# Attention: one unit in 15 of the 16 teams gets its exponentials on VectorE, in 20 steps spread over the team

## What is computed

```python
q = (x @ w_q.T).reshape(B, S, H, hd).transpose(0, 2, 1, 3)   # 16 heads of 16
...
scores = jnp.einsum('bhqd,bhkd->bhqk', q, k) / jnp.sqrt(jnp.float32(hd))
mask = prefix_lm_mask(NUM_PATCHES, S)                        # causal, first 196 keys open to the first 196 queries
scores = jnp.where(mask == 0, jnp.float32(-jnp.inf), scores)
attn = jax.nn.softmax(scores, axis=-1)
ctx = jnp.einsum('bhqk,bhkd->bhqd', attn, v)
```

## Time and profile before

| what | us |
|---|---|
| median of 3 runs (2373.08 to 2379.14) | 2374.06 |
| profiled execution, its own time | 2377.52 |
| its span | 2375.8 |
| start of the first and of the last exponential of attention | 217.1, 1252.8 |
| one team (start of the second to start of the third) | 64.7 |

### The profile page before, as it was taken

One profiled execution on the slowest core, in us unless ns is written; L12 is line 12 of the kernel. 1 busy time (PEld: TensorE's weight loads), 2 busy tenths in 40 slices (PEclk: granted clock), 3 DMA queues, 4 the chain that ended last, 5 costly groups with the idle time before them and its releaser, 6 DMA issues. The chain is left out here.

```text
span 2375.8 us, 37728 instructions
## 1 busy us (share of the span) xinstructions
PE 2127.9 (90%) x14197; PEld 1307.5 (55%) x14197; DVE 1303.1 (55%) x2070; ACT 1776.9 (75%) x2250; POOL 700.5 (29%) x700
## 2 busy tenths in 40 slices
PE   5995999999999999999995984999999999999920
PEld 4773333333333333333334873888888888888820
DVE  4663222222222222222224966988888888888848
ACT  4664999999999999999993762555566666666624
POOL 1111000000000000000001533887166666666631
PEclk9997999999999999999997976999999999999965
DMA  6886644555555544444503864888566767777558
GB/s 194 297 304 171 117 87 87 100 100 100 100 98 99 72 83 86 89 86 61 71 10 113 267 193 164 294 288 290 196 165 171 171 171 170 171 171 177 127 135 316
DMA packets 204264, 365.79 MB, mean 154 GB/s; under 512 B 18680, under 2 KB 141176, under 8 KB 195256
## 3 DMA queue, kind: packets, MB, share of 16 engines
q1 hardware_dynamic: 161084, 299.38, 46.9%
q0 software_dynamic: 34256, 55.20, 12.4%
q10 hardware_dynamic: 8748, 8.85, 1.2%
HBM read 219.81 MB, written 143.42 MB: 153 GB/s over the span
## 5 line engine op out<-in xcount | busy, mean ns | idle before, releaser
L959 ACT ACTIVATE att_prob<-att_scores 128x1024 f32<-128x1024 f32 (+2 forms) x1152 | 1022.6, 1047 | 38.2 <-PE att_scores L910 31.0
L929 PE MATMUL att_out<-att_prob,att_va 128*32 128x512 f32 (+3 forms) x5120 | 591.0, 543 | 14.7 <-DVE att_prob L991 14.7
L910 PEld LDWEIGHTS att_scores<-att_qs,att_ks 50*128 50x128 f32 x2560 | 213.1, 185 | 500.9 <-ACT att_prob L959 427.6
L910 PE MATMUL att_scores<-att_qs,att_ks 50*128 50x512 f32 (+3 forms) x2560 | 469.8, 433 | 18.3 <-DMA att_qs<-guard 17.0
L991 DVE SCALAR_TENSOR_TENSOR att_prob<-att_prob,att_tri 128x512 f32<-128x512 f32 x224 | 144.8, 688 | 613.4 <-ACT att_prob L959 613.4
L1485 POOL DMA_INDIRECT sums<-moe_y,moe_token x156 | 346.3, 2220 | 224.7 <-ACT moe_y L1641 189.1
L1548 PE MATMUL moe_ps<-moe_xt_hi,moe_w_hi 128*128 128x512 f32 x880 | 347.4, 395 | 0.0
L1548 PE MATMUL moe_ps<-moe_xt_hi,moe_w_lo 128*128 128x512 f32 x880 | 347.0, 394 | 0.0
L1548 PE MATMUL moe_ps<-moe_xt_lo,moe_w_hi 128*128 128x512 f32 x880 | 345.3, 392 | 0.0
L862 POOL DMA_DIRECT2D ctx_scr<-att_cout x64 | 48.3, 755 | 994.6 <-DVE att_cout L1009 954.1
L929 PEld LDWEIGHTS att_out<-att_prob,att_va 128*32 128x32 f32 x5120 | 111.3, 108 | 189.4 <-issue 96.3
(11 more groups left out here) (193 smaller groups left out, 3041.8 us busy)
## 6 DMA issues: line engine op xcount, KB each, us to landing
moe_wraw<-w_experts SPq DMA_DIRECT2D x55, 1412.0 KB, 6.6
qk_parts<-proj_qk SPq DMA_DIRECT2D x64, 512.0 KB, 4.2
att_qs<-qk_parts SPq DMA_DIRECT2D x180, 128.0 KB
att_ks<-qk_parts SPq DMA_DIRECT2D x180, 128.0 KB
rows_in<-att_zeros SPq DMA_DIRECT2D x13, 1548.0 KB, 21.0
moe_xin<-rows_in SPq DMA_DIRECT2D x39, 516.0 KB, 4.3
proj_xin<-x SPq DMA_DIRECT2D x16, 512.0 KB, 3.9
v_scr<-proj_va SPq DMA_DIRECT2D x16, 512.0 KB, 3.5
```

The lines of the kernel that those rows point to most:

```text
L910: last = nc.tensor.matmul(pss[e % SBUFS][:, h, at:at + CH - q0], ks[s][rows, half, kt * P:(kt + 1) * P], qs[s][rows, half, c * CH + q0:(c ...
L929: last = nc.tensor.matmul(pso[k % 2][strip, q0:], va[team % 2][:, kt, strip], prob[u % PBUFS][:, h, at:at + CH - q0], start=(kt == 0), sto ...
L959: nc.scalar.activation(prob[u % PBUFS][:, half * 2:half * 2 + 2, start:], pss[e % SBUFS][:, :, start:], ACT.Exp, scale=HD ** -0.5)\
```

## The change

`LATE` names unit 22, the second key tile of the last chunk, in teams 1 to 15. It leaves the ring of units. Its scores are computed behind those of unit 11, half a team earlier, in the same three score buffers and in turn with the others. Its two halves are not exponentiated on ScalarE: VectorE does it with 10 instructions for each half, 20 in all, as a power of two (scale and clamp out of PSUM, round, shift the integer part into the exponent, a polynomial of the fraction, and the product). `LATE_STEPS` hands out the 20: two each at units 11 to 16, one each at units 25 to 32. The result lies in a buffer of its own, `late_prob`. Its V comes behind V(33). A buffer of scores that VectorE reads is free again once step 0 of its half (`late_read`) is done. Behind the names below, "L" stands for this late unit: S(L,0), S(L,1), V(L).

```diff
+LATE = {UNITS.index((BCH - 1, ((1, 0, 0),), 0)): (11, (0, 1))}
+LATE_STEPS = {i: 2 for i in range(11, 17)} | {i: 1 for i in range(25, 33)}
+LATE_USED = NU - 3
...
+RING_UNITS = [team * NU + i for team in range(ALL_TEAMS) for i in range(NU) if i not in late(team)]
...
+    LATE_BEHIND[u] = [team * NU + m for m, (behind, _) in late(team).items() if behind == i]
+    SCORE_ORDER += [u] + LATE_BEHIND[u]
+    VALUE_ORDER += [u] + ([team * NU + m for m in late(team)] if i == LATE_USED else [])
...
+HALF_ORDER = [(u, half) for u in SCORE_ORDER for half in range(HALVES)]
...
+        def probs_of(u):
+            if u in RING_OF:
+                return prob[RING_OF[u] % PBUFS]
+            return late_prob[late_place[u % NU]]
+
...
+        def wait_probs_ready(eng, u):
+            for half in range(HALVES):
+                if (u, half) in EXPED_AT:
+                    eng.wait_ge(exped, EXPED_AT[u, half])
+                else:
+                    eng.wait_ge(late_done, VECTOR_AT[u, half] + 1)
+
+        def wait_scores_read(eng, e):
+
+            if e >= 0:
+                if HALF_ORDER[e] in EXPED_AT:
+                    eng.wait_ge(exped, EXPED_AT[HALF_ORDER[e]])
+                else:
+                    eng.wait_ge(late_read, VECTOR_AT[HALF_ORDER[e]] + 1)
...
-                        e = u * HALVES + half
-
-                        wait_from_one(pe, exped, e - SBUFS + 1)
+                        e = HALF_AT[u, half]
+
+                        wait_scores_read(pe, e - SBUFS)
...
+                for r in range(len(RING_UNITS) + TURN):
+                    if r < len(RING_UNITS):
+                        scores(RING_UNITS[r])
+                        for u in LATE_BEHIND[RING_UNITS[r]]:
+                            scores(u)
+                    if r >= TURN and RING_UNITS[r - TURN] in end_of:
+                        turn(end_of[RING_UNITS[r - TURN]])
+                    if 0 <= r - VALUES < len(RING_UNITS):
+                        u = RING_UNITS[r - VALUES]
+                        values(u)
+                        if u % NU == LATE_USED:
+                            for m in late(u // NU):
+                                values(u // NU * NU + m)
 
...
+                for u in SCORE_ORDER:
+                    wait_probs_free(act, u)
...
+                        if (u, half) in EXPED_AT:
+                            e = HALF_AT[u, half]
+                            act.wait_ge(scored, e + 1)
+                            nc.scalar.activation(probs_of(u)[:, half * 2:half * 2 + 2, start:],
+                                                 pss[e % SBUFS][:, :, start:], ACT.Exp, scale=HD ** -0.5)\
...
+                def power_of(u, half, side, stage):
+
+                    f, p, to = frac[side], poly[side], probs_of(u)[:, half * 2:half * 2 + 2]
+                    step, before = late_step[side], steps_done[side]
+                    if before and stage:
+                        dve.wait_ge(step, before)
+                    if stage == 0:
+                        e = HALF_AT[u, half]
+                        dve.wait_ge(scored, e + 1)
+                        if VECTOR_AT[u, LATE[u % NU][1][0]]:
+                            dve.wait_ge(late_done, VECTOR_AT[u, LATE[u % NU][1][0]])
+                        wait_probs_free(dve, u)
+                        V.tensor_scalar(f[:], pss[e % SBUFS][:], HD ** -0.5 * LOG2E, LOWEST, ALU.mult, ALU.max)\
+                            .then_inc(late_read, 1)
+                        return
+                    if stage == 1:
+                        dve.wait_ge(late_read, VECTOR_AT[u, half] + 1)
+                        done = V.tensor_scalar(p[:], f[:], ROUND, None, ALU.add)
+                    elif stage == 2:
+                        done = V.tensor_scalar(to.bitcast(I32), p[:].bitcast(I32), 23, None, ALU.logical_shift_left)
+                    elif stage == 3:
+                        done = V.scalar_tensor_tensor(f[:], p[:], ROUND, f[:], ALU.subtract, ALU.subtract)
+                    elif stage == 4:
+                        done = V.tensor_scalar(p[:], f[:], POWERS[-1], None, ALU.mult)
+                    elif stage < POLY - 1:
+                        done = V.scalar_tensor_tensor(p[:], p[:], POWERS[8 - stage], f[:], ALU.add, ALU.mult)
+                    else:
+                        V.scalar_tensor_tensor(to, p[:], 1.0, to, ALU.add, ALU.mult).then_inc(late_done, 1)
+                        return
+                    done.then_inc(step, 1)
+                    steps_done[side] += 1
 
                 def finish(k):
...
+                        for m, (behind, halves) in late(team).items():
+                            taken = sum(LATE_STEPS.get(b, 0) for b in range(i))
+                            for at in range(taken, taken + LATE_STEPS.get(i, 0)):
+                                stage, side = divmod(at, len(halves))
+                                power_of(team * NU + m, halves[side], side, stage)
```

More of the change, by code:

```diff
@@ L721, with late @@
 ALL_TEAMS = B * TEAMS
-ALL_UNITS = ALL_TEAMS * NU
+LATE = {UNITS.index((BCH - 1, ((1, 0, 0),), 0)): (11, (0, 1))}
+LATE_STEPS = {i: 2 for i in range(11, 17)} | {i: 1 for i in range(25, 33)}
+LATE_USED = NU - 3
+def late(team):
+    return LATE if team else {}
+RING_UNITS = [team * NU + i for team in range(ALL_TEAMS) for i in range(NU) if i not in late(team)]
+RING_OF = {u: r for r, u in enumerate(RING_UNITS)}
+SCORE_ORDER, VALUE_ORDER, LATE_BEHIND = [], [], {}
+for u in RING_UNITS:
+    team, i = divmod(u, NU)
+    LATE_BEHIND[u] = [team * NU + m for m, (behind, _) in late(team).items() if behind == i]
+    SCORE_ORDER += [u] + LATE_BEHIND[u]
+    VALUE_ORDER += [u] + ([team * NU + m for m in late(team)] if i == LATE_USED else [])
+USED_AT = {u: at + 1 for at, u in enumerate(VALUE_ORDER)}
+HALF_ORDER = [(u, half) for u in SCORE_ORDER for half in range(HALVES)]
+HALF_AT = {uh: e for e, uh in enumerate(HALF_ORDER)}
+BY_VECTOR = [(u, half) for u, half in HALF_ORDER if u not in RING_OF and half in LATE[u % NU][1]]
+BY_SCALAR = [uh for uh in HALF_ORDER if uh not in BY_VECTOR]
+EXPED_AT = {uh: at + 1 for at, uh in enumerate(BY_SCALAR)}
+VECTOR_AT = {uh: at for at, uh in enumerate(BY_VECTOR)}
+LOG2E = 1.4426950408889634
+LOWEST = -126.0
+ROUND = 1.5 * 2.0 ** 23 + 127.0
+POWERS = (-0.6931469775972935, 0.2402224208411893, -0.055507337459397184, 0.009671512697276688, -0.001326472638887228)
+POLY = 10
 def attend(nc, ident, norms, qk_parts, v_scr, guard, ctx_ch, rows_in, sums):
@@ L791, in attend @@
         prob = [ph.sb(f"prob{i}", [P, TEAM, CH]) for i in range(PBUFS)]
+        late_prob = [ph.sb(f"late_prob{i}", [P, TEAM, CH]) for i in range(len(LATE))]
+        frac = ph.sb2("frac", [P, 2, CH])
+        poly = ph.sb2("poly", [P, 2, CH])
         osb = ph.sb2("osb", [P, CH])
@@ L807, in attend @@
         scored, exped, masked, used = (ph.sem(n) for n in ("scores_ready", "probs_ready", "probs_masked", "probs_used"))
+        late_read, late_step, late_done = ph.sem("late_scores_read"), ph.sem2("late_steps"), ph.sem("late_probs_ready")
         o_copied, o_turned = ph.sem("out_copied"), ph.sem("out_turned")
@@ L828, in masked_to, with wait_probs_free @@
             return u // NU * masked_by[-1] + masked_by[u % NU]
+        late_place = {m: i for i, m in enumerate(LATE)}
+        def probs_of(u):
+            if u in RING_OF:
+                return prob[RING_OF[u] % PBUFS]
+            return late_prob[late_place[u % NU]]
+        def wait_probs_free(eng, u):
+            if u in RING_OF:
+                if RING_OF[u] >= PBUFS:
+                    eng.wait_ge(used, USED_AT[RING_UNITS[RING_OF[u] - PBUFS]])
+            elif u - NU in USED_AT and u - NU not in RING_OF:
+                eng.wait_ge(used, USED_AT[u - NU])
+        def wait_probs_ready(eng, u):
[10 more added lines that the diff above has]
+                    eng.wait_ge(late_read, VECTOR_AT[HALF_ORDER[e]] + 1)
         def load_guard(eng, team):
@@ L919, in values @@
                     k = team * BCH + c
-                    pe.wait_ge(exped, (u + 1) * HALVES)
+                    wait_probs_ready(pe, u)
                     if masks(u):
@@ L929, in values @@
                             last = nc.tensor.matmul(pso[k % 2][strip, q0:], va[team % 2][:, kt, strip],
-                                                    prob[u % PBUFS][:, h, at:at + CH - q0], start=(kt == 0),
+                                                    probs_of(u)[:, h, at:at + CH - q0], start=(kt == 0),
                                                     stop=(i == LAST_UNIT[c]), skip_group_check=True)
@@ L951, in _ @@
                 load_guard(act, 0)
-                for u in range(ALL_UNITS):
-                    wait_from_one(act, used, u - PBUFS + 1)
+                for u in SCORE_ORDER:
+                    wait_probs_free(act, u)
                     start = UNITS[u % NU][2]
                     for half in range(HALVES):
[L957 to L961, removed]
```

(19 more changed lines are left out.)

## The result

The changed kernel takes 2427.97 us (median of 4, 2426.06 to 2429.78) against 2376.02 us before (4 runs): slower by 52 us, ratio 1.0213, 95% interval 1.02 to 1.0226. The forecast had the sign and most of the mechanism, but counted only 29 us.

A forecast was written before the change was run, and what follows sets the result against it. ScalarE's exponentials were taken to bound plain stretches, TensorE's queue the chunk ends. Stall 3.05 plus V(L) 0.7 less removed work 1.83 gave 1.92 us a team, 28.8 over 15 teams: 2403 us predicted, range 2388 to 2422.

The forecast's parts named there:

- What bounds the kernel: In attention, ScalarE's exponentials set the pace in plain units; at chunk ends TensorE's queue and its waits do.
- Removed work: Two exponentials of 128 x 1024 fewer on ScalarE in each of 15 teams: gain of 1.83 us a team.
- The chain V(9), copy, read, S(12,1): Amid the team, S(12,1) waits for VectorE's first read, queued behind the copy that waits for V(9): loss 3.05 us.
- the SBUF row: Scale-and-clamp with both sides in SBUF, 0.719 us: lower end for VectorE's read, taken as 1.20; loss would be 2.57.
- The two rows that the size came from: For VectorE's read: copy out of PSUM, 1.195 us, and scale-and-clamp within SBUF, 0.719; said to differ in the PSUM operand.
- V(L) at the end: Between V(33) and the next team's S(0), V(L) takes 0.99 us on TensorE: loss taken as 0.7 us a team.
- The other 18 steps: VectorE's steps for L after the two reads cost nothing, under cover of its idle time, ending ahead of the masks.
- The sum of these: Attention's net loss: 3.05 + 0.7 - 1.83 = 1.92 us a team, times 15 = 28.8 us.
- the clock: Rival, chance 0.20: TensorE's clock falls in the stall amid the team; 2417 us with half the teams, 2431 with all.
- If it comes right behind the stall: A clock fall there makes S(12,1), turn and V(10) take up to twice as long: 1.7 to 2.0 us more a team.

The follow-up runs named there:

- Experiment 7: Changed kernel with S(L,0) scored behind S(13,0), S(L,1) behind S(14,0), and V(L) behind V(30), all 20 VectorE steps kept: 2364.23 us, ratio 0.9944 to before.
- Experiment 6: Changed kernel with VectorE's read of the first half of L ahead of the copy of chunk 1 instead of behind it: 2380.2 us, ratio 1.0009 to before.
- experiment 2: Changed kernel's order alone: both exponentials of L stay on ScalarE, VectorE does none of the 20 steps: 2393.74 us, ratio 1.0067 to before.
- experiments 3: Changed kernel with S(L) behind S(10) instead of S(11), and the first 12 VectorE steps at units 10 to 15: 2374.52 us, ratio 0.9992 to before.
- Experiment 5: Changed kernel with further matmuls in both TensorE waits, two ahead of S(L,1) and seven ahead of S(12,1): 2404.86 us, ratio 1.0106 to before.
- experiment 1: Changed kernel with four further matmuls between S(12,0) and S(12,1) of teams 1 to 15: 2413.7 us, ratio 1.0161 to before.

## Why the prediction was wrong

The terms of the sum can be read one by one from the starts of exponentials, in the changed kernel's team without a fall (the third) and in the teams before:

| us | before | after | difference | forecast |
|---|---|---|---|---|
| amid the team, E(9) to E(13) | 6.94 | 10.02 | +3.08 | +3.05 |
| E(13) to E(33), with unit 22 gone | 36.00 | 34.26 | -1.74 | -1.83 |
| the team's end, E(33) to the next E(3) | 10.75 | 11.33 | +0.58 | +0.7 |

- **What bounds the kernel: right.** Plain units keep their pace, and the loss lies where TensorE's queue decides.
- **Removed work, -1.83 us a team: right.** It measured 1.74. Experiment 7 shows that it is there to be had: 0.94 us a team came through as gain.
- **The chain V(9), copy, read, S(12,1): right.** 4.68 us measured against 4.72. Experiment 6 takes one link out and the wait is gone. The read was sized rightly, 1.215 us in the mean of 30; the SBUF row would have been wrong. The two rows that the size came from differ in the operation too, not in the PSUM operand alone as the prediction says; the changed kernel's steps settle it, where a TENSOR_SCALAR of 128 x 1024 takes 0.68 us within SBUF and 1.215 out of PSUM.
- **V(L) at the end, 0.7 us: a little high.** It measured 0.58, in experiment 2 too; the 0.73 that the order costs there holds another 0.15 from amid the team.
- **The other 18 steps, nothing: right.** Their cover held; experiments 3 and 7 do all of them. The shift on integers took 0.777 us, not 0.72, without effect.
- **The sum of these, 1.92 us a team: right, to the hundredth by luck.** The three terms are off by 0.03, 0.09 and 0.12 and their errors cancel. 66.63 us a team with both waits filled against 64.70 is 1.93; and 2404.86 us is next to the 2403 forecast, though over the before of its own set it is 26 us and not 28.8.
- **The step that failed is the clock, a term that the sum of 1.92 us a team put at nothing and left to a rival.** "If it comes right behind the stall" had 0.20, and within it I took half of the teams. It came in 14 of 15. The forecast counted the time that S(12,1) waits, but not what the wait does to the work behind it. The price, put at 1.7 to 2.0 us, measured 1.57 in the chain shown above and 1.48 in the mean of the teams. With both, 15 x 1.92 + 13 x 1.48 + 2.69 is 51 us, and 52 was measured. Experiment 5, which takes the falls away and leaves S(12,1) as late as it was, shows that 23 to 26 of the 52 us were the clock's. The range ended at 2422 for the same reason. I had seen both idle times in the chain and named them; what I did not do is count how little TensorE was busy across them together, 1.53 of 3.40 us, and ask whether any stretch of attention before had been that empty.

Open is why the one team kept its clock with the same two waits, and why five teams of experiment 1 did not with a shorter one. In the changed kernel the falls follow each other at 68.27 us, whatever the length of the team between, and come early or late behind the waits accordingly; so more than the waits themselves has a part in it, and no run here shows what.

## What to carry to other kernels

When work moves to an idle engine, look for what it holds there and in which order: here VectorE had 48 us free in each team, and the loss came from one read queued behind a copy, and from two of three buffers held at once. One buffer at a time, taken where the receiving engine has nothing ahead of it, turned 52 us lost into 14 gained. And a new wait on TensorE can be priced twice, once as a wait and once by the clock behind it, as the two waits of 0.68 and 1.52 us were and the single new one of 0.69 us was not; a few matmuls without use inside the wait show which part is which.

## What the hardware showed that I had not expected

Waits of 0.68 and 1.52 us, with 1.5 us of work between them, were followed by 3.4 us at half the granted clock in 13 teams and 6.8 us in one. In experiment 2 waits of 0.68 (once 0.98) and 0.33 us did it too, in six teams, and in nine they did not. In experiment 1, with the longer wait cut to 0.59 us, five teams still had it. With the first read moved (experiment 6) the wait of 0.69 us ahead of S(L,1) brought no fall in any team, though a wait of 0.36 us for a mask ends 2.7 us before its own end. So the falls that were read here had two new waits ahead of them, whose ends lie 1.8 or 3.0 us apart; but two such waits do not always bring a fall.
